# Sorting edges in a graph network: a key's count from a sum of sign times step in place of a lookup of its own, and equal keys of a lane counted ahead of the loop

## What is computed

```python
def _denoise_gcn_layer(x, row, col, noise, nbW, nbb, selfW, selfb, attW, attb):
    f1 = x[row]
    f2 = x[col]
    h1 = relu(f1 @ nbW + nbb)
    h2 = relu(f2 @ selfW + selfb)
    log_alpha = concatenate([h1, h2], axis=1) @ attW + attb
    u = clip(noise, EPS_NOISE, 1.0 - EPS_NOISE)
    gate = sigmoid(log(u) - log1p(-u) + log_alpha)
    mask = clip(gate * (ZETA - GAMMA) + GAMMA, 0.0, 1.0)[:, 0]
    rowsum = segment_sum(mask, row, num_segments=N_NODES) + EPS_DEG
    d_inv_sqrt = clip(rowsum ** (-0.5), 0.0, 10.0)
    vals = mask * d_inv_sqrt[row] * d_inv_sqrt[col]
    return segment_sum(vals[:, None] * f2, row, num_segments=N_NODES)
```

## Time and profile before

| | |
|---|---|
| median of 3 runs | 6455.31 us (6450.32 to 6471.18) |
| the profiled execution | 6455.86 us, of which the span is 6454.1 us |
| busy in the span | VectorE 82%, TensorE 69%, ScalarE 39%, GpSimd 19% |
| DMA | 1160.68 MB, mean 180 GB/s |

### The profile page before, as it was taken

The page is one execution under the profiler, slowest core; times in us unless marked ns, Lnnn a source line. Parts: engine busy times, 40 slices in busy tenths (PEclk is TensorE's granted clock), DMA queues, the critical chain, the costliest instruction groups (busy, mean ns, idle before and its releaser), DMA issues. The chain is left out here.

```text
span 6454.1 us, 166440 instructions
## 1 busy us (share of the span) xinstructions
PE 4433.2 (69%) x58388; PEld 3992.8 (62%) x58388; DVE 5279.6 (82%) x10519; ACT 2500.7 (39%) x5126; POOL 1241.8 (19%) x1562
## 2 busy tenths in 40 slices
PE   3777777775878887355556767978885455557766
PEld 2666666664468887344446666578885354446666
DVE  8999999996459998899976666079998999966666
ACT  2666666662345554355520000445553455510000
POOL 0000000000013333000025444023332000035444
PEclk9777777775555555677778898555555667778888
DMA  2000000000456665799979988066665899979998
GB/s 67 0 0 0 0 0 0 0 0 9 12 190 232 233 234 169 260 333 333 332 245 250 248 245 233 0 216 231 232 233 161 286 332 331 333 232 252 250 251 227
DMA packets 438061, 1160.68 MB, mean 180 GB/s; under 512 B 211241, under 2 KB 216974, under 8 KB 437402
## 3 DMA queue, kind: packets, MB, share of 16 engines
q1 hardware_dynamic: 316671, 549.99, 27.3%
q0 software_dynamic: 75264, 354.33, 20.1%
q10 hardware_dynamic: 46036, 255.30, 10.4%
HBM read 936.26 MB, written 281.94 MB: 189 GB/s over the span
## 5 line engine op out<-in xcount | busy, mean ns | idle before, releaser
L1585 PE MATMUL psG<-y_window,area 128*128 128x64 bf16 x14976 | 678.2, 218 | 769.7 <-DVE area L1233 612.3
L1585 PEld LDWEIGHTS psG<-y_window,area 128*128 128x128 bf16 x14976 | 634.2, 115 | 814.0 <-issue 500.9
L1598 PE MATMUL psG<-work,edge 112*128 112x192 bf16 x7104 | 770.2, 277 | 393.2 <-DVE edge L1268 392.8
L1598 PEld LDWEIGHTS psG<-work,edge 112*128 112x128 bf16 x7104 | 726.7, 150 | 436.0 <-DVE edge L1268 350.2
L580 POOL DMA_INDIRECT work<-msg_d,widx x444 | 543.7, 1225 | 2063.6 <-issue 1633.9
L636 ACT ACTIVATE work<-iota,work 128x149 bf16<-128x149 f32 x2496 | 788.9, 406 | 0.0
L1407 PE MATMUL psG<-area,work 128*128 128x112 bf16 x2496 | 551.3, 390 | 337.7 <-DVE area L965 337.7
L1407 PEld LDWEIGHTS psG<-area,work 128*128 128x128 bf16 x2496 | 357.7, 149 | 486.3 <-issue 342.3
L1400 PE MATMUL psG<-work,merge 128*128 128x148 bf16 x4992 | 544.4, 293 | 69.8 <-ACT work L636 69.8
L1400 PEld LDWEIGHTS psG<-work,merge 128*128 128x128 bf16 x4992 | 527.7, 132 | 92.2 <-issue 66.3
L1268 DVE TENSOR_TENSOR edge<-y_edge,ids 112x2048 bf16<-112x2048 int16 x444 | 524.8, 1223 | 23.1
(11 more groups left out here) (254 smaller groups left out, 8330.7 us busy)
## 6 DMA issues: line engine op xcount, KB each, us to landing
msg_d<-work ACTq DMA_DIRECT2D x312, 784.0 KB, 4.6
area<-rlo_d SPq DMA_DIRECT2D x312, 512.0 KB, 4.2
merge<-crel_d SPq DMA_DIRECT2D x312, 512.0 KB, 5.0
area<-crelp_d SPq DMA_DIRECT2D x312, 512.0 KB, 5.7
y_window<-y_d SPq DMA_DIRECT2D x312, 48.0 KB, 3.7
work<-msg_d,widx POOLq DMA_INDIRECT x444, 10.0
y_d<-cur SPq DMA_DIRECT2D x7, 1008.0 KB, 3.8
y_d<-work SPq DMA_DIRECT2D x7, 1008.0 KB, 4.8
```

The source lines that it names most:

```text
L1585: ins = pe.matmul(psG[:, 2 * h + k // CH, k % CH * D:(k % CH + 1) * D], col_one_hots[:, h, k * P:(k + 1) * P], y_window[:, h, m * D:(m + 1 ...
L1598: ins = pe.matmul(psG[:, slot_, 0:MW], q_one_hots[slot_][0:WP, g, :, s], windows[slot_][0:WP, g, s, 0:MW], start=g == 0 and s == 0, stop=g ...
```

## The change

A pair's lookup is replaced. ScalarE now copies all 128 lanes of the starts from PSUM to `start_all` in SBUF, with a zero in front. VectorE takes the differences of neighbouring keys (`rise`, fp16), multiplies them with the signs of all 16 keys of a lane at once (`picks`, fp16, rows at a pitch of 150), adds the halves of the rows (first fold), a quarter more (second fold), and reduces the remaining 40 columns. Half of that sum, with a constant ST in one of the two extra columns, is the start at the key. `dup` for all supersteps is made ahead of the loop, from 15 shifted comparisons and additions. The sign buffers become four, so the loops of the three engines run over four supersteps a round; the order within them is as before. Several tiles move to other places of the same SBUF areas.

```diff
-        below = words(0, 2384).bitcast(bf16).rearrange("p (h k n) -> p h k n", h=2, k=CT)
+        SB, CB = 150, 2
+        below = words(0, 2 * CT * SB).bitcast(bf16).rearrange("p (b k n) -> p b k n", b=4, k=CT)
+        rise = scratch[:, 1616:1616 + HB].bitcast(f16).rearrange("p (h n) -> p h n", h=2)
+        start_all = flat_merge[:, 1600:1600 + 2 * HS].rearrange("p (h n) -> p h n", h=2)
+        start_row = start_all[0:1, :, 1:HS]
+        dup = key
+        dup_new = area[:, 0:NC // 2].bitcast(bf16)
+        equal = area[:, NC // 2:NC].bitcast(bf16).rearrange("p (t k) -> p t k", k=CT)
+        picks = area[:, RECS * CT * CT:RECS * CT * CT + CT * (CB + HB)].bitcast(f16).rearrange("p (h k n) -> p h k n", h=2, k=CT)
...
-            def start(i, h):
-                act.wait_ge(starts_counted, i * 2 + h + 1)
-                wait(act, start_row_stored[h], i * 16)
-                act.activation(start_row[0:1, h, :], psG[0:1, h, 0:HB], ACT.Copy, bias=float(ST // 2)).then_inc(start_row_ready, 1)
+            def start(t, h):
+                act.wait_ge(starts_counted, t + 1)
+                wait(act, rise_ready, t - 1)
+                wait(act, start_row_stored[h], (t - h) * 8)
+                act.activation(start_all[:, h, 1:HS], psG[:, h, 0:HB], ACT.Copy, bias=float(ST // 2)).then_inc(start_row_ready, 1)
...
-            def mark_side(t, h):
-                wait(act, starts_counted, t - 1)
+            def mark_side(t, b):
+                wait(act, starts_counted, t - 3)
+                wait(act, signs_taken, t - 3)
                 for k in range(CT):
-                    ins = act.activation(below[:, h, k, :], iota_all[:, :], ACT.Sign, bias=keyf[:, bass.ds(t * CT + k, 1)], scale=-1.0)
+                    ins = act.activation(below[:, b, k, 0:HS], iota_all[:, :], ACT.Sign, bias=keyf[:, bass.ds(t * CT + k, 1)], scale=-1.0)
                 ins.then_inc(below_ready, 1)
...
+            def sort_four(i):
+                for b in range(4):
+                    t, h = i * 4 + b, b % 2
+                    start(t, h)
+                    if not isinstance(i, int) or t >= 2:
+                        keep_records(t - 2, h)
+                    if not isinstance(i, int) or t + 2 < T:
+                        mark_side(t + 2, (b + 2) % 4)
...
-            link(dve.tensor_scalar(lower, lower, 0.0, None, ALU.is_gt))
...
-            link(dve.tensor_scalar(iota_half, iota_all[:, 0:HB], 0.5, None, ALU.add))
+            by_step, dup_step = key.rearrange("p (t k) -> p t k", k=CT), dup_new.rearrange("p (t k) -> p t k", k=CT)
+            link(dve.memset(dup_new, 0.0))
+            for d in range(1, CT):
+                link(dve.tensor_tensor(equal[:, :, 0:CT - d], by_step[:, :, d:CT], by_step[:, :, 0:CT - d], ALU.is_equal))
+                link(dve.tensor_tensor(dup_step[:, :, d:CT], dup_step[:, :, d:CT], equal[:, :, 0:CT - d], ALU.add))
+            link(dve.tensor_copy(dup, dup_new))
+            link(dve.memset(start_all[:, :, 0:1], 0.0))
+            link(dve.memset(picks[:, :, :, 0:1], float(ST)))
+            link(dve.memset(picks[:, :, :, 1:2], 0.0))
+            dve.wait_ge(base_loaded, 16)
...
-                step(1, dve.tensor_tensor(alike, keys.unsqueeze(3).to_broadcast([P, 2, CT, CT]), keys.unsqueeze(2).to_broadcast([P, 2, CT, CT]), ALU.is_equal))
-                step(2, dve.tensor_tensor(alike_before, alike, lower.unsqueeze(1).to_broadcast([P, 2, CT, CT]), ALU.mult))
-                step(3, dve.tensor_reduce(dup.rearrange("p (u k) -> p u k", u=2), alike_before, AX.X, ALU.add))
                 for h in range(2):
                     t = i * 2 + h
                     dve.wait_ge(start_row_ready, t + 1)
-                    for k in range(CT):
-                        ins = dve.scalar_tensor_tensor(picks[h][:, k, :], iota_half, keyf[:, bass.ds(t * CT + k, 1)], psG[:, h, 0:HB],
-                                                       ALU.is_equal, ALU.mult, accum_out=picked[:, h * CT + k:h * CT + k + 1])
-                    ins.then_inc(keys_picked, 1)
-                dve.wait_ge(keys_picked, i * 2 + 2)
-                step(4, dve.scalar_tensor_tensor(position, picked, float(ST // 2), dup, ALU.add, ALU.add))
+                    dve.tensor_tensor(rise[:, h, :], start_all[:, h, 1:HS], start_all[:, h, 0:HB], ALU.subtract).then_inc(rise_ready, 1)
+                    dve.wait_ge(rise_ready, t + 1)
+                    dve.tensor_tensor(picks[:, h, :, CB:CB + HB], below[:, 2 * v + h, :, 0:HB], rise[:, h, :].unsqueeze(1).to_broadcast([P, CT, HB]), ALU.mult).then_inc(signs_taken, 1)
+                dve.wait_ge(signs_taken, i * 2 + 2)
+                step(1, dve.tensor_tensor(picks[:, :, :, CB:half], picks[:, :, :, CB:half], picks[:, :, :, half:CB + HB], ALU.add))
+                step(2, dve.tensor_tensor(picks[:, :, :, CB:CB + quarter], picks[:, :, :, CB:CB + quarter], picks[:, :, :, half - quarter:half], ALU.add))
+                dve.tensor_reduce(picked.rearrange("p (u k) -> p u k", u=2), picks[:, :, :, 0:half - quarter], AX.X, ALU.add).then_inc(keys_picked, 1)
+                dve.wait_ge(keys_picked, i + 1)
+                step(3, dve.scalar_tensor_tensor(position, picked, 0.5, dup[:, bass.ds(i * 2 * CT, 2 * CT)], ALU.mult, ALU.add))
...
-            def count_starts(t, h):
+            def count_starts(t, h, b):
                 pe.wait_ge(below_ready, t + 1)
-                wait(pe, keys_picked, t - 1)
                 wait(pe, start_row_ready, t - 1)
...
-                        ins = pe.matmul(psG[:, h, 0:HB], sides[:, s, :], below[:, h, k, s:s + HB], start=s == 0 and k == 0, stop=s == 1 and k == CT - 1)
+                        ins = pe.matmul(psG[:, h, 0:HB], sides[:, s, :], below[:, b, k, s:s + HB], start=s == 0 and k == 0, stop=s == 1 and k == CT - 1)
...
+                    if not isinstance(i, int) or t + 2 < T:
+                        count_starts(t + 2, h, (b + 2) % 4)
+                    move_records(t, h)
```

More of the change, by code:

```diff
@@ L59, in build @@
 def build(nc, x, src, dst, noise, params, out):
-    f32, bf16, i32, u16, i16 = mybir.dt.float32, mybir.dt.bfloat16, mybir.dt.int32, mybir.dt.uint16, mybir.dt.int16
+    f32, bf16, f16, i32, u16, i16 = mybir.dt.float32, mybir.dt.bfloat16, mybir.dt.float16, mybir.dt.int32, mybir.dt.uint16, mybir.dt.int16
     ALU, ACT, AX = mybir.AluOpType, mybir.ActivationFunctionType, mybir.AxisListType
@@ L157, in build @@
         iota_j = merge_bf[:, HS * CT:HS * CT + CT * CT].rearrange("p (j k) -> p j k", k=CT)
-        lower = merge_bf[:, HS * CT + CT * CT:HS * CT + 2 * CT * CT].rearrange("p (k m) -> p k m", m=CT)
         sides = merge_bf[:, HS * CT + 2 * CT * CT:HS * CT + 2 * CT * CT + 2 * P].rearrange("p (s n) -> p s n", s=2)
-        iota_half = flat_merge[:, 1600:1600 + HB]
-        below = words(0, 2384).bitcast(bf16).rearrange("p (h k n) -> p h k n", h=2, k=CT)
[L162 to L170, removed]
+        SB, CB = 150, 2
+        below = words(0, 2 * CT * SB).bitcast(bf16).rearrange("p (b k n) -> p b k n", b=4, k=CT)
+        place = words(4800, 2048).bitcast(bf16).rearrange("p (h n k) -> p h n k", h=2, k=CT)
+        slot_of = scratch[:, 1200:1456].bitcast(bf16).rearrange("p (u j k) -> p u j k", u=2, j=CT)
+        lane_slot = scratch[:, 1456:1488].bitcast(bf16).rearrange("p (s n) -> p s n", s=2)
+        picked, position = scratch[:, 1488:1520], scratch[:, 1520:1552].bitcast(i32)
+        lane_slot_int = scratch[:, 1552:1616].bitcast(i32).rearrange("p (s n) -> p s n", s=2)
+        rise = scratch[:, 1616:1616 + HB].bitcast(f16).rearrange("p (h n) -> p h n", h=2)
[4 more added lines that the diff above has]
+        equal = area[:, NC // 2:NC].bitcast(bf16).rearrange("p (t k) -> p t k", k=CT)
         keyf = words(HI * D - NC, NC)
@@ L174, in build @@
         temps = [words(i * NC, NC) for i in range(2)]
-        spread_rec = bcast[:, :, :].rearrange("p a e -> p (a e)")[:, 0:2 * RECS * CT * CT].bitcast(bf16).rearrange("p (h m j k) -> p h m j k", h=2, m=RECS, j=CT)
-        picks = [t.bitcast(bf16).rearrange("p (k n) -> p k n", k=CT) for t in (scratch[:, 0:CT * HB // 2], words(5700, CT * HB // 2))]
+        spread_rec = area[:, 0:RECS * CT * CT].bitcast(bf16).rearrange("p (h m j k) -> p h m j k", h=2, m=RECS, j=CT)
+        picks = area[:, RECS * CT * CT:RECS * CT * CT + CT * (CB + HB)].bitcast(f16).rearrange("p (h k n) -> p h k n", h=2, k=CT)
         ends = scratch[0:1, 1200:1200 + 2 * NS].rearrange("p (m t u) -> p m t u", m=2, u=2)
@@ L279, in build @@
         ends_stored, ends_loaded, base_ready, base_stored, base_loaded = (sem(n) for n in ("ends_stored", "ends_loaded", "base_ready", "base_stored", "base_loaded"))
-        keys_ready, below_ready, starts_counted, keys_picked, start_row_ready = (sem(n) for n in ("keys_ready", "below_ready", "starts_counted", "keys_picked", "start_row_ready"))
```

(40 more changed lines are left out.)

4 lines of the change are left out of this document (1 added, 3 removed).

## The result

The changed kernel took 6559.31 us (median of 4 runs, 6557.63 to 6571.87) beside 6456.56 us for the kernel before (4 runs, 6450.32 to 6471.18). The ratio is 1.0146 with a 95% interval of 1.0123 to 1.0168, so it is slower by 79 to 108 us. The forecast was +83 us and 6539.

What follows compares the result with a forecast made beforehand. The prediction took a closed ring of waits across VectorE, TensorE and ScalarE, period 17.80 us, to bound the sort loop. +58 in the loop and +25 ahead of it gave +83, 6539 us, range 6510 to 6595 with run spread.

Steps and rivals of the forecast that it cites:

- The ring: Sort loop: spread_rec of h = 0, move, keep_records, signs, start of h = 1, VectorE's steps, spread_rec again; period 17.80 us.
- What is removed: VectorE, before start of h = 1 arrives: equal-key comparison (2.1 us) and 16 picks of h = 0, worth nothing.
- The five steps: VectorE between start of h = 1 and the position: rise, product, two folds, reduce; 5.50 us replacing 4.75.
- The 9.38 that was to stay: From spread_rec's end of h = 0 through move, keep_records, signs and start to h = 1's picks: 9.38 us, unchanged.
- the forecast of 0.75 a pair: Growth of the sort loop's period from 17.80 to 18.55 us, over 78 pairs 58.5 us; bounds 0.6 to 1.1.
- The part ahead of the loop: VectorE's added clearing, 15 shifts, copy and memsets: net 28.7 us, 3.8 hidden, so +25; +20 to +44.
- The Trainium skill's rule on alignment: Odd shifts ahead of the loop: two elements a cycle need 4-byte alignment, so 10 us more, +93 for +83.
- The signs to look for: Profile afterwards: move every 18.5 us, some 5 us idle before rise of h = 1, VectorE about 70%, first count about 131.
- The product at the slow rate: Rival: bf16 times fp16 product on VectorE has no packed form, 1.23 us more a pair, 6635 us; chance 0.06.
- Five steps 0.3 us shorter than the picks: Rival: by unseen overlap the steps on VectorE take 4.43 us, balancing the prologue, 6456 us; chance 0.04.
- over 1.1 us a pair more on the ring: Rival: a second wait or slow odd forms add more to the loop, 6600 us or so; chance 0.03.
- VectorE as the bound, relieved: Rival: VectorE's 13.0 us a pair sets the loop if start of h = 1 comes within 3.9 us; 6107; chance 0.05.

Runs made afterwards that it cites:

- e1: Changed kernel with one swap on ScalarE, mark_side(t + 2) ahead of keep_records(t - 2): 6444.32 us, 0.9956 of the kernel before.
- e5: Changed kernel with both starts of a pair ahead of all signs on ScalarE, both counts ahead of both moves on TensorE: 6127.15 us, 0.9473.
- e3: Changed kernel with an extra reduction of 1280 elements on VectorE behind the product of h = 0: 6556.96 us, 1.013 of the kernel before.
- e4: Changed kernel with the same extra reduction of 1280 elements behind the product of h = 1: 6664.69 us, 1.0306 of the kernel before.
- e8: Changed kernel with ten more comparisons ahead of the loop, varying row length and an operand's begin: 6581.95 us in one run.
- the last form: Changed kernel in e5's order, with keys_ready raised ahead of the equal keys and start_all's zero column cleared before that: 6113.51 us, 0.9453.

## Why the prediction was right, point by point

- **What bounds the kernel.** Right. The ring was read from a wait of 0.5 us on an engine that was 94% busy in the loop. e1 shows that the signs were on it, and e5 that with the move out of it too VectorE waits for nobody. e3 and e4 show that the same work counts behind `start` of h = 1 and not ahead of it.
- **What is removed is off the ring.** Right: the pick of h = 0 and the comparison of equal keys went, and all that came of it is idle time, 5.5 us a pair.
- **The five steps.** Forecast 0.35 + 1.42 + 1.42 + 0.79 + 1.52 = 5.50, measured 5.64. The durations are right to 0.01 us, the mix of bf16 and fp16 included. What I missed is 0.13 more in the wait ahead of the position (0.16 for 0.03). The first two and the last two pairs stand outside the loop and read `dup` at a fixed address. There the wait is 0.03 and the five steps take 5.51 us, as in these rows of the first pair:

```profile
148.63 1.49 DVE L964 TENSOR_REDUCE area<-area 128x32 f32<-128x1280 f16 x1
150.15 0.19 DVE L966 SCALAR_TENSOR_TENSOR area<-area,edge 128x32 int32<-128x32 f32 x1
```

In the 74 pairs inside the loop the address comes from a register, and the trace has an instruction for registers (FUSED_REGOPS, 0.075 us) ahead of L966 in each.
- **The 9.38 that was to stay.** It became 9.25 in the pair shown, and this is the same piece. Before, the first pick of h = 1 read its key at an address from a register; it started 0.43 us after `start` did in the loop, and 0.30 in the first pair, outside the loop. `rise` has a fixed address and starts 0.31 after `start`. So the register work left one place of the ring and came back at another. I saw neither, and the forecast of 0.75 a pair met the measured 0.756 (over 77 periods) because the two are alike in size; that part is luck. The loop grew by 58.1 us for 58.
- **The part ahead of the loop.** The direction was right, the term mis-sized: 28.4 for 25. The fault is in the shifts: 29.7 us from 102.59 to 132.27 for 25.1. The eight odd shifts took 17.6 us where the sum had 13.4, the seven even ones 12.1 for 11.7. In odd shifts the rate of the two-byte rows doesn't hold (e8), nor does a plain slow rate. The clearing was shorter, 1.10 for 2.13, since it went out as half as many four-byte elements, and so was the copy, 0.81 for 1.46. These 1.7 us hide part of the miss.
- **The Trainium skill's rule on alignment.** I let the sum go by the rate of the aligned rows. The Trainium skill's VectorE: DVE Perf Modes, "Mode 2×_1P", was nearer in that alignment matters, but the measured price of an odd begin is some 0.16 us for 156 rows of an even length from 4 to 14 elements, not a fall to half the rate, and odd lengths cost by themselves. By that rule the odd shifts would take 10 us more than my sum; they took 4.2 more. The Trainium skill's Vector Engine (DVE) Microarchitecture Reference, section 5.1, "4-byte alignment makes no difference", doesn't hold for these rows of an even length from 2 to 14 elements.
- **The sum.** +83 forecast, +103 between the medians, with an interval of 79 to 108. 86.5 us of it lie before the end of the sort. The rest is in stages that the change doesn't touch, and no run explains it.
- **The signs to look for.** A move every 18.55 us for 18.5, an idle stretch of 5.5 us for some 5, VectorE busy for 67% of the loop for about 70%, the first count at 135.5 for 131.
- **The rivals.** The product at the slow rate: its 1.39 us rule it out. Five steps 0.3 us shorter than the picks, or over 1.1 us a pair more on the ring: 0.756 a pair lies between. VectorE as the bound, relieved: refuted for this order, and right for another. Its 13.0 us a pair and its condition came true in e5, at 6127 us, near the 6107 it gave.

## What to carry to other kernels

Before giving an engine less to do, follow one round of the loop from an instruction to the same instruction of the next round, through every wait, however short. If such a ring adds up to the period, only work on it counts, and a step that is cheaper in total but longer behind the last wait makes the loop slower. An issue order that puts work of the next round behind a result of this one is often what closes the ring: here the change alone cost 1.5%, a new order alone gave 0.8%, and both together gave 5.3%, with 5.5% in the last form.

## What the runs showed of the hardware

- A tensor_tensor of bf16 times fp16 into fp16, with one operand broadcast over 16 rows, ran at the rate of all-bf16 ones: 2368 elements in 1392 ns.
- Over short rows a two-byte tensor_tensor depends on row length and begin. Of 156 rows, lengths 3, 5, 7 and 8 all took 0.81 to 0.83 us, length 6 took 0.65, length 4 0.48, length 2 0.44; an operand one element in added 0.16 to lengths 4, 6, 12 and 14, 0.04 to length 2, and nothing to lengths 3, 5 and 7.
- A VectorE instruction that waited for the one before it started 0.03 us after that one's end where its operands had fixed addresses (position, pairs outside the loop), and 0.16 us after it where one had an address from a register (the same instruction, pairs inside the loop).
- Sixteen matmuls of 112 columns took 3.55 us at a granted clock of 0.50 and 3.51 at 0.97, while 32 of 148 columns took 4.13 at 0.50 and 2.30 at 1.00. The operands of the first are read with a stride of 16 elements, those of the second (signs and `sides`) without; that the stride is the reason was not tested.
